# Down and output projections of a float32r macaron block: high and low weights side by side, one 512-column product for the high block

## The chip, the cores and the metric

One NeuronCore of a Trainium2 chip runs the whole kernel in one launch. The metric is device time in microseconds (us), the median of repeated executions. One further execution was recorded by the hardware profiler; its trace is what the rows below come from.

Engines are named as the profile names them: PE is TensorE's matmul side and PEld its weight loads, DVE is VectorE, ACT is ScalarE, POOL is GpSimd, SP is SyncE (here it only issues DMAs). A matmul takes a stationary block (the "weights" of PEld, up to 128x128) and streams a moving block of up to 512 columns past it.

## The reference

The input x is 4096 tokens of 256 channels. The block is `x + 0.5*FFN(LN(x))`, then `x + Attention(LN(x))`, then `x + 0.5*FFN(LN(x))` again. FFN is a mixture of 8 experts with top-2 routing and a capacity of 1228 rows per expert:

```python
h = einp2 @ w_c_fc + b_c_fc            # (1228 x 256) @ (256 x 1024), per expert
g = einp2 @ w_gate + b_gate
o = silu(h * g) @ w_c_proj + b_c_proj  # (1228 x 1024) @ (1024 x 256): the down projection
```

Attention is a gated linear recurrence over 16 heads of 64 channels, `S = a*S + k v^T`, `o = q S`, whose output is multiplied by `W_o` (1024 x 256): the output projection. All is float32.

## The kernel before

**Split precision.** Each float32 operand of a large product is split into a high part, rounded to the float32r type by an ACT copy, and a low part, the remainder, made by a DVE subtraction. A product of two such operands is three matmuls into the same PSUM bank: high x high, high x low, low x high. The helper `passes` (line 298) lists them in that order.

**Stages.** Round r=0: `route` (normalise, logits, top-2, scatter of rows into `expert_in` in HBM), then a loop over eight experts; then `attention`; then round r=1 with `route` and eight experts again; then `combine_last`, in which POOL gathers expert rows and DVE adds them into x, and SP stores x.

**One expert.** Its 1228 rows are three groups of 512, 512 and 204 rows. The second group is computed 384 or 512 wide (`wide1`), the third only if it holds rows (`last_group`); both are read at run time from `long`. `up` (line 552) makes 8 units per group, 12 matmuls each, into banks 0 to 3; ACT and DVE turn them into `s_hi` and `s_lo`. `down` (line 571) makes tiles of 128 rows: tile t has 4+4+2 = 10 numbers per expert (the last has 76 rows), and for each of the HJ=8 blocks j of the hidden axis it issues three matmuls with 256 columns each, 24 matmuls per tile, into columns 0 to 255 of bank 4 + t%2. The stationary block is the 128x128 block of `s_hi` or `s_lo`, the moving one 256 columns of `pr_hi` or `pr_lo`. The order on PE is `up` 0, `up` 1, `down` 0 (tiles 0 to 3), `up` 2 if it exists, `down` 1 tiles 0 and 1 (t = 4, 5), `turn` of the next expert's first rows (line 539), t = 6, then t = 7 only if `wide1`, then t = 8, 9 only if `last_group`, then the next expert's `up` 0.

**The bank's way back.** When a tile is done PE raises `y_done`; DVE's `y_out` (line 1205) adds bank and bias into `y_sb` (one addition, line 1212) and raises `y_copied`. PE needs that before it writes tile t+2 into the same bank (line 582); SP needs it to store the tile (line 357), and behind stores 0 to 3 SP issues the next expert's row loads (line 383). DVE's stream is in order. Behind tile 6 stand two `split_fc` subtractions (line 1165) and the two subtractions of `turned` (line 1177), and these raise `xt_split`, for which the next expert's first matmul waits (line 556); `y_out(7)` to `y_out(9)` come after them.

**Attention.** A loop over eight supertiles of 4 tiles of 128 tokens. At the end of each, `out_projection` (line 721) makes 4 tiles of 24 matmuls with 256 columns (8 head pairs g, three passes) into banks 3 and 4, and DVE's `add_output` (line 1374) adds each bank into x with one addition and raises `wo_added`. Then PE goes on with `values` of the next supertile (48 matmuls with 512 columns) and waits for the last `wo_added` behind them (line 763).

The weights sit in `halves`, a buffer of 32768 float32r per partition: `pr_hi` at 8192 and `pr_lo` at 10240; `wo` at 16384 and 18432.

Of the kernel before, what the change touches and what calls it, by code (L numbers as in the profile page):

```python
# [20 lines left out]
ALU = mybir.AluOpType  # L21
# [8 lines left out]
P = 128  # L30
T = 4096
C = 256
# [65 lines left out]
def macaron(nc, x_in, w_q, w_k, w_v, w_gate, b_gate, w_o, router_w, router_b,  # L98
            w_fc, b_fc, w_g, b_g, w_proj, b_proj, out):
    with ExitStack() as ctx:  # L100
# [39 lines left out]
        def part(t, at, *dims):  # L140
            n = 1
            for d in dims:
                n *= d
            v = t[:, at:at + n]
            names = "abc"[:len(dims)]
            if len(dims) == 1:
                return v
            return v.rearrange(f"p ({' '.join(names)}) -> p {' '.join(names)}",
                               **{names[i]: dims[i] for i in range(1, len(dims))})
# [13 lines left out]
        fc_hi, fc_lo, gw_hi, gw_lo = (part(halves, 2048 * i, KC, HID) for i in range(4))  # L163
        pr_hi, pr_lo = (part(halves, 2048 * i, HJ, C) for i in (4, 5))
        s_hi = [part(halves, 12288 + 8192 * i, HJ, 512) for i in range(2)]
# [40 lines left out]
                          for i in range(4))  # L206
        wo = [part(halves, 16384, NPAIR, C), part(halves, 18432, NPAIR, C)]
        xa = [part(halves, 20480, KC, SW), part(halves, 21504, KC, SW)]
# [44 lines left out]
        y_done = sem("y_done")  # L253
        y_copied = sem("y_copied")
        y_stored = [sem("y_stored0"), sem("y_stored1")]
# [18 lines left out]
        o_done, ot_hi_made, ot_split = sem("o_done"), sem("ot_hi_made"), sem("ot_split")  # L274
        wo_done, wo_added = sem("wo_done"), sem("wo_added")
        stored = sem("stored")
# [219 lines left out]
        def _(pe):  # L496
# [74 lines left out]
            def down(r, e, n, tiles=range(SUPER)):  # L571
                u = r * E + e
                buf = n % 2
                pe.wait_ge(s_split, u * UNITS + (n + 1) * HJ)
                if n == 0:
                    pe.wait_ge(proj_split, u * 4 + 4)
                for i, (o, m) in enumerate(GROUP_TILES[n]):
                    if i not in tiles:
                        continue
                    t = 4 * n + i  # L580
                    if t >= 2:
                        pe.wait_ge(y_copied, u * Y_TILES + t - 1)
                    ps = [(j, a, v) for j in range(HJ)
                          for a, v in passes((s_hi[buf], s_lo[buf]), (pr_hi, pr_lo))]
                    for k, (j, a, v) in enumerate(ps):
                        mm = pe.matmul(bank[4 + t % 2][0:m, 0:C], a[:, j, o:o + m], v[:, j, :],  # L586
                                       start=(k == 0), stop=(k == len(ps) - 1))
                    mm.then_inc(y_done, 1)
# [37 lines left out]
            def attention():  # L626
# [94 lines left out]
                def out_projection(s):  # L721
                    pe.wait_ge(ot_split, s * NPAIR + NPAIR)
                    for b in range(SUPER):
                        if b >= 2:
                            pe.wait_ge(wo_added, s * SUPER + b - 1)
                        ps = [(g, a, v) for g in range(NPAIR) for a, v in passes(ot, wo)]
                        for i, (g, a, v) in enumerate(ps):
                            m = pe.matmul(bank[3 + b % 2][:, 0:C], a[:, g, b * P:(b + 1) * P], v[:, g, :],  # L728
                                          start=(i == 0), stop=(i == len(ps) - 1))
                        m.then_inc(wo_done, 1)  # L730
# [57 lines left out]
        def _(act):  # L788
# [27 lines left out]
            def split_attention(n):  # L816
                w = (wq, wk, wz, wv, wo)[n]
                act.wait_ge(aw_staged[n], 16)
                copy(w[0].rearrange("p a n -> p (a n)"), raw_w[n]).then_inc(aw_hi_made, 1)

# [184 lines left out]
        def _(dve):  # L1005
# [161 lines left out]
            def split_attention(n):  # L1167
                w = (wq, wk, wz, wv, wo)[n]
                dve.wait_ge(aw_hi_made, n + 1)
                v.tensor_tensor(w[1].rearrange("p a n -> p (a n)"), raw_w[n],  # L1170
                                as_f32(w[0].rearrange("p a n -> p (a n)")), ALU.subtract).then_inc(aw_split, 1)

# [8 lines left out]
            def expert(r, e, last):  # L1181
# [23 lines left out]
                def y_out(t):  # L1205

                    n = t // 4 if t < 8 else 2
                    m = GROUP_TILES[n][t - 4 * n][1]
                    dve.wait_ge(y_done, u * Y_TILES + t + 1)

                    dve.wait_ge(y_stored[t % 2], (u * (Y_TILES // 2) + t // 2 + 1) * 16)
                    v.tensor_tensor(y_sb[0:m, t % 2, :], bank[4 + t % 2][0:m, 0:C], y_bias[0:m, :],  # L1212
                                    ALU.add).then_inc(y_copied, 1)

# [55 lines left out]
            def attention():  # L1270
# [103 lines left out]
                def add_output(s, b):  # L1374
                    i = s * SUPER + b
                    dve.wait_ge(wo_done, i + 1)
                    v.tensor_tensor(tile_of(x, i), bank[3 + b % 2][:, 0:C], tile_of(x, i),
                                    ALU.add).then_inc(wo_added, 1)

# [85 lines left out]
```

## Time and profile before

| what | value |
|---|---|
| median of 3 runs | 2385.33 us (2384.83 to 2389.75) |
| the profiled execution's own time | 2385.95 us |
| its span, first to last instruction | 2384.2 us |
| PE busy / PEld busy | 2025.1 us (85%) / 1799.6 us (75%) |
| DVE / ACT / POOL busy | 1263.0 us (53%) / 1130.6 us (47%) / 298.3 us (13%) |
| mean granted TensorE clock | 0.944 of full speed |
| matmuls, in all / of line 586 (down) / of line 728 (output projection) | 13967 / 3288 / 768 |

A row of a timeline gives the start, the duration, the engine, the line and operation, what it writes and reads, how many instructions were merged into the row, and in brackets how long the engine had been idle before and what released it. Merged instructions overlap: an instruction's duration includes its latency, so the distance between starts is what an engine pays for one. A matmul's "busy" time in a table by lines is the time its kind occupied the engine, while the mean of one is its latency.

### The profile page before, as it was taken

What the parts mean: (1) busy time and instruction counts of PE and PEld (TensorE: products, weight loads), DVE (VectorE), ACT (ScalarE), POOL (GpSimd) and SP (SyncE); (2) the same over time, 40 slices, a digit from 0 to 9 for tenths busy, and PEclk for the clock granted to TensorE, in tenths of its full rate; (3) what the DMA queues carried; (4) which work ended last, traced back from release to release, by engine and by line L of the source; (5) the groups of instructions that cost most, each with busy time, mean ns of one, the idle gap of its engine ahead of it and who ended that gap; (6) DMA issues with size and microseconds to landing.
All of it is one profiled execution on the core that took longest, in us unless ns stands there. A gap on an engine that the chain in (4) does not pass through costs nothing.

```text
span 2384.2 us, 38690 instructions
## 1 busy us (share of the span) xinstructions
PE 2025.1 (85%) x13967; PEld 1799.6 (75%) x13968; DVE 1263.0 (53%) x3160; ACT 1130.6 (47%) x2054; POOL 298.3 (13%) x332
## 2 busy tenths in 40 slices
PE   5169999999995989898988999983399999999990
PEld 5158889898985777787877788873398899988890
DVE  6345555555455647474564756545254545564544
ACT  1055566655453535354453644520366556665540
POOL 1720000000002101110010110006300000000226
PEclk9999999999997999999999999975699999999995
DMA  6242221222121000000000000002411221222224
GB/s 259 103 144 81 97 86 55 71 97 97 37 87 53 15 11 11 14 12 13 10 10 10 14 13 0 1 1 91 158 52 69 93 80 48 73 91 97 76 60 142
DMA packets 95402, 150.90 MB, mean 63 GB/s; under 512 B 9583, under 2 KB 76678, under 8 KB 94068
## 3 DMA queue, kind: packets, MB, share of 16 engines
q1 hardware_dynamic: 83008, 116.46, 14.3%
q0 software_dynamic: 12288, 32.91, 4.4%
q8 instruction: 81, 1.33, 0.2%
q14 instruction: 25, 0.20, 0.0%
HBM read 98.84 MB, written 51.15 MB: 63 GB/s over the span
## 4 chain that ended last, share of the span: by engine, by line
PE 66%; DVE 11%; PEld 7%; issue 6%; POOL 6%; ACT 2%; DMA 1%; PEldq 1%; DVEq 0%; POOLq 0%; SPq 0%; ACTq 0%
PE bank L567 27%; PE bank L586 12%; PE bank L638 5%; PE bank L728 4%; PEld bank L586 4%; POOL expert_in L436 4%; PE bank L662 4%; PEld bank L567 3%; PE bank L682 2%; DVE wide L1343 2%; PE bank L716 2%; POOL halves L443 2%; PE bank L531 2%; PE bank L708 2%; DVE wide L1366 1%
## 5 line engine op out<-in xcount | busy, mean ns | idle before, releaser
L567 PE MATMUL bank<-halves 128*128 128x512 f32 (+2 forms) x3744 | 770.4, 366 | 22.3 <-DVE halves L1177 22.3
L567 PEld LDWEIGHTS bank<-halves 128*128 128x128 f32 x3744 | 648.9, 191 | 128.0 <-issue 24.6
L586 PE MATMUL bank<-halves 128*128 128x256 f32 (+1 forms) x3288 | 403.2, 283 | 3.0 <-issue 3.0
L586 PEld LDWEIGHTS bank<-halves 128*128 128x128 f32 (+1 forms) x3288 | 397.3, 189 | 5.7 <-issue 4.8
L834 ACT ACTIVATE temp<-bank,bias_now 128x512 f32<-128x512 f32 (+1 forms) x312 | 200.3, 642 | 367.6 <-PE bank L567 367.3
L1190 DVE SCALAR_TENSOR_TENSOR temp<-bank,bias_fc,temp 128x512 f32<-128x512 f32 (+1 forms) x312 | 216.3, 693 | 225.9 <-ACT temp L834 222.4
L638 PE MATMUL bank<-halves 128*128 128x512 f32 x1152 | 290.4, 404 | 2.0 <-DVE halves L1317 2.0
L1197 DVE TENSOR_TENSOR halves<-temp,halves 128x512 fp32r<-128x512 f32 (+1 forms) x312 | 198.1, 635 | 126.6 <-ACT halves L790 123.5
L638 PEld LDWEIGHTS bank<-halves 128*128 128x128 f32 x1152 | 215.6, 192 | 51.1 <-DVE halves L1317 2.4
L790 ACT ACTIVATE halves<-temp 128x512 fp32r<-128x512 f32 (+1 forms) x313 | 184.9, 591 | 10.0
L443 POOL DMA_INDIRECT halves<-expert_out,read_slot x96 | 104.2, 1085 | 672.7 <-DMA expert_out<-rows 648.0
L1325 DVE TENSOR_TENSOR_SCAN wide<-wide,limit 128x64 f32<-128x64 f32 x512 | 100.6, 270 | 154.1 <-ACT wide L909 154.1
L1212 DVE TENSOR_TENSOR rows<-bank,rows 128x256 f32<-128x256 f32 (+1 forms) x160 | 66.9, 423 | 217.7 <-PE bank L586 191.6
L841 ACT ACTIVATE temp<-temp 128x512 f32<-128x512 f32 (+1 forms) x312 | 179.9, 577 | 0.2
L790 ACT ACTIVATE halves<-wide 128x512 fp32r<-128x512 f32 (+1 forms) x196 | 115.5, 644 | 116.7 <-DMA wide<-in_L_ffn_w_gate 99.0
L790 ACT ACTIVATE temp<-wide 64x256 f32<-64x256 f32 (+1 forms) x192 | 105.9, 551 | 130.7 <-DVE wide L1366 128.4
L790 ACT ACTIVATE halves<-bank 128x512 fp32r<-128x512 f32 (+1 forms) x176 | 89.4, 541 | 162.7 <-PE bank L548 127.6
L548 PE MATMUL bank<-ident,wide 128*128 128x128 f32 x320 | 43.3, 276 | 125.0 <-DMA wide<-expert_in 125.0
L436 POOL DMA_INDIRECT expert_in<-wide,temp x128 | 127.7, 998 | 145.0 <-issue 82.3
L548 PEld LDWEIGHTS bank<-ident,wide 128*128 128x128 f32 x320 | 38.0, 144 | 129.7 <-DMA wide<-expert_in 126.0
L1165 DVE TENSOR_TENSOR halves<-wide,halves 128x512 fp32r<-128x512 f32 x128 | 81.8, 685 | 86.2 <-ACT halves L790 78.1
L465 POOL COPY temp<-carry 128x384 f32<-128x384 f32 x64 | 32.3, 505 | 704.0 <-DVE wide L1343 704.0
(155 smaller groups left out, 2124.2 us busy)
## 6 DMA issues: line engine op xcount, KB each, us to landing
expert_out<-rows SPq DMA_DIRECT2D x144, 128.0 KB, 1.7
wide<-in_L_ffn_w_c_fc SPq DMA_DIRECT2D x16, 1024.0 KB, 5.4
wide<-in_L_ffn_w_gate SPq DMA_DIRECT2D x16, 1024.0 KB, 7.6
wide<-in_L_ffn_w_c_proj SPq DMA_DIRECT2D x16, 1024.0 KB, 5.4
wide<-expert_in SPq DMA_DIRECT2D x32, 512.0 KB, 4.9
expert_in<-halves SPq DMA_DIRECT2D x9, 1024.0 KB
x<-in_L_attn_x SPq DMA_DIRECT2D x4, 1024.0 KB, 9.3
out_x<-x SPq DMA_DIRECT2D x32, 128.0 KB, 2.5
```

The lines of the kernel that those rows point to most:

```text
L436: pool.indirect_dma_start(expert_in, bass.IndirectOffsetOnAxis(ap=write_slot[:, j:j + 1], axis=0), xn[:, i, :], None, bounds_check=ROWS - ...
L443: pool.indirect_dma_start(into, None, expert_out, bass.IndirectOffsetOnAxis(ap=read_slot[:, j:j + 1], axis=0)).then_inc(landed, 16)
L567: m = pe.matmul(bank[at + b][:, 0:w], a[:, kc, j * P:(j + 1) * P], v[:, kc, 0:w], start=(i == 0), stop=(i == len(ps) - 1))
L586: mm = pe.matmul(bank[4 + t % 2][0:m, 0:C], a[:, j, o:o + m], v[:, j, :], start=(k == 0), stop=(k == len(ps) - 1))
L638: m = pe.matmul(bank[at][:], a[:, kc, g * P:(g + 1) * P], v[:, kc, :], start=(i == 0), stop=(i == len(ps) - 1))
L662: m = pe.matmul(bank[5 + n % 2][:], a[:, kc, b * P:(b + 1) * P], v[:, kc, half * 512:(half + 1) * 512], start=(i == 0), stop=(i == len(ps) ...
L790: return nc.scalar.activation(o, i, ACT.Copy)
L834: nc.scalar.activation(g_sb[b][:, 0:w], bank[2 + b][:, 0:w], ACT.Identity, bias=bias_now[:, j:j + 1]).then_inc(g_copied, 1)
L841: nc.scalar.activation(hg[b][:, 0:w], hg[b][:, 0:w], ACT.Silu).then_inc(silu_made, 1)
L1190: v.scalar_tensor_tensor(hg[b][:, 0:w], bank[b][:, 0:w], bias_fc[:, bass.ds(col, 1)], g_sb[b][:, 0:w], ALU.add, ALU.mult).then_inc(hg_made, 1)
L1197: v.tensor_tensor(s_lo[buf][:, j, 0:w], hg[b][:, 0:w], as_f32(s_hi[buf][:, j, 0:w]), ALU.subtract).then_inc(s_split, 1)
L1325: ins = v.tensor_tensor_scan(gates, gates, limit[:], 0.0, ALU.add, ALU.min)
```

## The change

The high and low weights of the down projection are stored next to each other for each hidden block j (256 high columns, then 256 low), and so are those of the output projection for each head pair g. The high stationary block meets both in one matmul with 512 columns, which fills the whole bank: columns 0 to 255 collect high x high, columns 256 to 511 collect high x low. The low stationary block still meets the high weights with 256 columns, into columns 0 to 255. So a block j or g has two matmuls in place of three, with the same 768 columns in all. DVE reads both halves of the bank: it adds the first half to the bias (or to x), waits for that on a semaphore of its own, and adds the second half. `y_copied` and `wo_added` are raised by the second addition. The subtractions and copies that make the weights' parts keep their sizes; they write rows of 256 with a stride of 512.

```diff
-        pr_hi, pr_lo = (part(halves, 2048 * i, HJ, C) for i in (4, 5))
+        pr = part(halves, 8192, HJ, 2, C)
+        pr_hi, pr_lo = pr[:, :, 0, :], pr[:, :, 1, :]
...
-        wo = [part(halves, 16384, NPAIR, C), part(halves, 18432, NPAIR, C)]
+        wo_both = part(halves, 16384, NPAIR, 2, C)
+        wo = [wo_both[:, :, 0, :], wo_both[:, :, 1, :]]
...
-                    ps = [(j, a, v) for j in range(HJ)
-                          for a, v in passes((s_hi[buf], s_lo[buf]), (pr_hi, pr_lo))]
-                    for k, (j, a, v) in enumerate(ps):
-                        mm = pe.matmul(bank[4 + t % 2][0:m, 0:C], a[:, j, o:o + m], v[:, j, :],
-                                       start=(k == 0), stop=(k == len(ps) - 1))
+                    y_bank = bank[4 + t % 2]
+                    for j in range(HJ):
+                        pe.matmul(y_bank[0:m, :], s_hi[buf][:, j, o:o + m], pr[:, j, :, :].rearrange("p a n -> p (a n)"),
+                                  start=(j == 0), stop=False, skip_group_check=True)
+                        mm = pe.matmul(y_bank[0:m, 0:C], s_lo[buf][:, j, o:o + m], pr_hi[:, j, :],
+                                       start=False, stop=(j == HJ - 1), skip_group_check=True)
...
-                        ps = [(g, a, v) for g in range(NPAIR) for a, v in passes(ot, wo)]
-                        for i, (g, a, v) in enumerate(ps):
-                            m = pe.matmul(bank[3 + b % 2][:, 0:C], a[:, g, b * P:(b + 1) * P], v[:, g, :],
-                                          start=(i == 0), stop=(i == len(ps) - 1))
+                        o_bank = bank[3 + b % 2]
+                        for g in range(NPAIR):
+                            pe.matmul(o_bank[:], ot[0][:, g, b * P:(b + 1) * P],
+                                      wo_both[:, g, :, :].rearrange("p a n -> p (a n)"),
+                                      start=(g == 0), stop=False, skip_group_check=True)
+                            m = pe.matmul(o_bank[:, 0:C], ot[1][:, g, b * P:(b + 1) * P], wo[0][:, g, :],
+                                          start=False, stop=(g == NPAIR - 1), skip_group_check=True)
...
-                    v.tensor_tensor(y_sb[0:m, t % 2, :], bank[4 + t % 2][0:m, 0:C], y_bias[0:m, :],
-                                    ALU.add).then_inc(y_copied, 1)
+                    y, y_bank = y_sb[0:m, t % 2, :], bank[4 + t % 2]
+                    v.tensor_tensor(y, y_bank[0:m, 0:C], y_bias[0:m, :], ALU.add).then_inc(y_halved, 1)
+                    dve.wait_ge(y_halved, u * Y_TILES + t + 1)
+                    v.tensor_tensor(y, y_bank[0:m, C:2 * C], y, ALU.add).then_inc(y_copied, 1)
...
                     v.tensor_tensor(tile_of(x, i), bank[3 + b % 2][:, 0:C], tile_of(x, i),
+                                    ALU.add).then_inc(wo_halved, 1)
+                    dve.wait_ge(wo_halved, i + 1)
+                    v.tensor_tensor(tile_of(x, i), bank[3 + b % 2][:, C:2 * C], tile_of(x, i),
                                     ALU.add).then_inc(wo_added, 1)
```

## Rows read from the trace of the kernel before

**Rows 1.** The page: span, and each engine's busy time, share and instructions.
```profile
span 2384.2 us, 38690 instructions
PE 2025.1 (85%) x13967; PEld 1799.6 (75%) x13968; DVE 1263.0 (53%) x3160; ACT 1130.6 (47%) x2054; POOL 298.3 (13%) x332
```
**Rows 2.** The page: chain of work that ended last, by engine and by line.
```profile
PE 66%; DVE 11%; PEld 7%; issue 6%; POOL 6%; ACT 2%; DMA 1%; PEldq 1%; DVEq 0%; POOLq 0%; SPq 0%; ACTq 0%
PE bank L567 27%; PE bank L586 12%; PE bank L638 5%; PE bank L728 4%; PEld bank L586 4%; POOL expert_in L436 4%; PE bank L662 4%; PEld bank L567 3%; PE bank L682 2%; DVE wide L1343 2%; PE bank L716 2%; POOL halves L443 2%; PE bank L531 2%; PE bank L708 2%; DVE wide L1366 1%
```
**Rows 3.** Groups by line, PE: shapes, count, busy us, mean ns, idle before.
```profile
L586 PE MATMUL bank<-halves 128*128 128x256 f32 x3120 | 383.6, 284 | 3.0 <-issue 3.0
L728 PE MATMUL bank<-halves 128*128 128x256 f32 x768 | 96.1, 287 | 11.4 <-DVE halves L1371 11.4
L586 PE MATMUL bank<-halves 128*76 128x256 f32 x168 | 20.7, 278 | 0.0
```
**Rows 4.** Timelines: what follows tiles of 256, 512, 384 and 204 columns.
```profile
2317.78 0.42 DVE L1212 TENSOR_TENSOR rows<-bank,rows 128x256 f32<-128x256 f32 x1 [2.46 <-PE bank L586]
2320.66 0.42 DVE L1212 TENSOR_TENSOR rows<-bank,rows 128x256 f32<-128x256 f32 x1 [2.45 <-PE bank L586]
...
873.77 0.60 ACT L790 ACTIVATE wide<-bank 128x512 f32<-128x512 f32 x1 [0.76 <-PE bank L662]
875.13 0.60 ACT L790 ACTIVATE wide<-bank 128x512 f32<-128x512 f32 x1 [0.76 <-PE bank L662]
...
2062.13 0.69 ACT L834 ACTIVATE temp<-bank,bias_now 128x512 f32<-128x512 f32 x1 [0.20 <-PE bank L567]
2064.21 0.69 ACT L834 ACTIVATE temp<-bank,bias_now 128x512 f32<-128x512 f32 x1 [0.20 <-PE bank L567]
...
717.62 0.43 ACT L834 ACTIVATE temp<-bank,bias_now 128x204 f32<-128x204 f32 x1 [0.24 <-PE bank L567]
718.96 0.43 ACT L834 ACTIVATE temp<-bank,bias_now 128x204 f32<-128x204 f32 x1 [0.24 <-PE bank L567]
```
**Rows 5.** Lines 1212 and 1250: durations min/median/max; a dependent pair of line 1250.
```profile
L1212 DVE TENSOR_TENSOR rows<-bank,rows x160: 414/424/425, 194.8 to 2323.5; 128x256 f32<-128x256 f32 x144, 76x256 f32<-76x256 f32 x16
L1250 DVE SCALAR_TENSOR_TENSOR x<-halves,weight,x x64: 457/483/489, 750.3 to 1431.9; 128x256 f32 x56, 128x256 f32<-128x256 f32 x8
750.32 1.01 DVE L1250 SCALAR_TENSOR_TENSOR x<-halves,weight,x 128x256 f32<-128x256 f32 x2
```
**Rows 6.** Timeline, 278 to 281 us: from tile 6 to the next expert.
```profile
278.06 0.42 DVE L1212 TENSOR_TENSOR rows<-bank,rows 128x256 f32<-128x256 f32 x1 [2.21 <-PEq L620]
278.40 1.28 DVE L1165 TENSOR_TENSOR halves<-wide,halves 128x512 fp32r<-128x512 f32 x2
279.60 1.28 DVE L1177 TENSOR_TENSOR halves<-bank,halves 128x512 fp32r<-128x512 f32 x2
281.02 2.50 PE L567 MATMUL bank<-halves 128*128 128x512 f32 x5 [3.09 <-DVE halves L1177]
```
**Rows 7.** Waits of PE: us in total, times, longest.
```profile
PE bank L567 <- DVE halves L1177: 22.3, 11, 3.1
```
**Rows 8.** Stretches: busy us per engine, then granted clock (third value from the end).
```profile
280.60:284.00 3.40, 2.98 (x7) 2.41 (x8) 1.37 (x4) 0.00 (x0) 0.00 (x0) 0.50 0.23 77
347.10:353.90 6.80, 6.80 (x30) 5.65 (x31) 1.90 (x5) 1.72 (x3) 0.00 (x0) 1.00 0.35 103
2164.80:2171.60 6.80, 5.62 (x13) 4.45 (x14) 2.13 (x5) 0.10 (x1) 0.00 (x0) 0.50 0.25 72
```
**Rows 9.** Timelines behind the last projection of each of the three stages.
```profile
742.42 1.52 POOL L443 DMA_INDIRECT halves<-expert_out,read_slot  x1 [607.20 <-DMA expert_out<-rows]
1589.28 3.03 PE L509 MATMUL bank<-ident,wide 128*128 128x128 f32 x13 [5.59 <-DVE wide L1122]
2323.80 12.74 DVE L1261 SCALAR_TENSOR_TENSOR x<-wide,weight,x 128x256 f32<-128x256 f32 x32
2326.97 10.40 POOL L443 DMA_INDIRECT halves<-expert_out,read_slot  x1 [40.84 <-DMA expert_out<-rows]
```
**Rows 10.** Row loads of the next expert (line 334) and the turn they feed.
```profile
203.83 1.00 SPq L334 DMA_DIRECT2D wide<-expert_in  x2
DMA to landing us min/median/max: 4.6/4.9/5.3
208.79 0.93 PE L548 MATMUL bank<-ident,wide 128*128 128x128 f32 x7
```

More of the change, by code:

```diff
@@ L144, in part @@
             v = t[:, at:at + n]
-            names = "abc"[:len(dims)]
+            names = "abcd"[:len(dims)]
             if len(dims) == 1:
@@ L253, in macaron @@
         y_done = sem("y_done")
-        y_copied = sem("y_copied")
+        y_halved, y_copied = sem("y_halved"), sem("y_copied")
         y_stored = [sem("y_stored0"), sem("y_stored1")]
@@ L274, in macaron @@
         o_done, ot_hi_made, ot_split = sem("o_done"), sem("ot_hi_made"), sem("ot_split")
-        wo_done, wo_added = sem("wo_done"), sem("wo_added")
+        wo_done, wo_halved, wo_added = sem("wo_done"), sem("wo_halved"), sem("wo_added")
         stored = sem("stored")
@@ L818, in split_attention @@
                 act.wait_ge(aw_staged[n], 16)
-                copy(w[0].rearrange("p a n -> p (a n)"), raw_w[n]).then_inc(aw_hi_made, 1)
+                copy(w[0], raw_w[n].rearrange("p (a n) -> p a n", a=w[0].shape[1])).then_inc(aw_hi_made, 1)
             def turned(r, e, n):
@@ L1169, in split_attention @@
                 dve.wait_ge(aw_hi_made, n + 1)
-                v.tensor_tensor(w[1].rearrange("p a n -> p (a n)"), raw_w[n],
-                                as_f32(w[0].rearrange("p a n -> p (a n)")), ALU.subtract).then_inc(aw_split, 1)
+                v.tensor_tensor(w[1], raw_w[n].rearrange("p (a n) -> p a n", a=w[0].shape[1]),
+                                as_f32(w[0]), ALU.subtract).then_inc(aw_split, 1)
             def turned(r, e, n):
```

## The prediction

> **What bounds the kernel now.** I read the shares first: PE is busy for 85% of the span, DVE for 53% [rows 1]. The chain that ended last runs through PE and PEld for 73% of the span, and the two changed lines hold 20% of it (586: 12% and 4%, 728: 4%) [rows 2]. So time saved on PE in these lines is mostly time saved, and the question is how much each instruction pays beside its columns. The groups by line give the amount of work: 3120 + 168 matmuls in line 586, 768 in line 728, nearly without idle time before them (3.0 and 11.4 us) [rows 3]. At 24 a tile that is 137 down tiles and 32 output tiles, 169 in all. The counts also tell the experts apart: 168/24 = 7 tiles have 76 rows, so 7 of the 16 experts have a third group; 137 - 16*7 - 2*7 = 11 have tile 7; 9 experts have no third group, 4 of them with tile 7 and 5 without.
>
> **What one matmul costs.** A matmul's mean latency (284 ns) says nothing of this; the distance between tiles does. Down tiles of 24 matmuls with 256 columns follow each other at 2320.66 - 2317.78 = 2.88 us, 120.0 ns each. The value products are 6 matmuls with 512 columns in 1.36 us, 226.7 ns each. The units 384 wide, 12 matmuls in 2.08 us, pay 173.3 ns; those 204 wide, 12 in 1.34 us, pay 111.7 ns [rows 4]. From 256 to 384 to 512 the price rises by 53.3 ns for 128 columns each time, 0.417 ns a column, so a matmul pays 13.3 ns besides its columns (120.0 - 256*0.417). At 204 columns the line would give 98 ns, and the row says 112: something else, the next weight load most likely, holds it there. At 256 columns, 8 ns above that floor, the columns still decide.
>
> **What the change removes.** Three matmuls at 120.0 become one at 226.7 and one at 120.0: 360.0 becomes 346.7, 13.3 ns less for each of 8 blocks, 0.107 us a tile. All 169 tiles: 18.0 us. The trace has no stretch in which the two widths alternate, so this is bounded from both sides. At most nothing but columns is paid: 768*0.417 = 320 ns, 40 ns a block, 54 us in all. At least nothing is gained (360), if the wide product pays as much as the two it stands for; a loss would need a price above 226.7 for a 512-column matmul that has a weight load behind it, and line 662 is nothing but such matmuls. I take 346.7, since both its terms are the neighbouring rows' own prices for exactly these shapes.
>
> The Trainium skill ("TensorE: Matmul & The Clock Gate", section "Back-to-back issue gap") gives an isolated matmul N/2.4 + 2.5 ns, 109 ns for 256 columns and 216 for 512; by that the third instruction is worth 2.5 ns, 3.4 us in all. The rows stand 11 ns above it at both widths, so here the measured 13.3 decides.
>
> **What it adds on DVE, where covered.** One more addition per tile. The second one depends on the first: in line 1250's dependent pairs, two additions of 483 ns take 1.01 us together, so the second starts about 0.04 us after the first has ended; an addition of line 1212 takes 0.424 us [rows 5]. The pair therefore ends 0.46 us later than the single one did. Inside a run of tiles this costs nothing: PE needs the bank only after a whole further tile (2.77 us), the pair is back in about 1.1 us, and DVE had been idle for 2.45 us before each addition [rows 4]. Behind the third group's units and in the supertiles it is also covered: line 1377's last addition has the 48 value products (11 us) before PE waits for it. The copies and subtractions of the weights keep their element counts: nothing.
>
> **Where it is not covered.** (1) The nine expert boundaries without a third group. Behind tile 6 stand, in DVE's order, y_out(6), two subtractions of line 1165 and two of line 1177, and PE's next expert waits for the last: 278.06 to 280.88 on DVE, and PE goes on at 281.02 after 3.09 us [rows 6]. Of the eleven such waits [rows 7] two are the first experts of the rounds, nine are these. The additional 0.46 us lies fully in this chain: 9*0.46 = 4.1 us. In four of them PE does tile 7 meanwhile, and that tile's 0.107 us is lost in the longer wait: 0.4 us. (2) The ends of three stages: the gathers after round 0 wait for the last stored tile, PE's first transposes of round 1 wait for DVE, and DVE's 32 additions of line 1261 and POOL's gathers follow the very last tile [rows 9]. Each shifts by 0.46: 1.4 us. (3) SP issues the next expert's row loads behind store 3. Relative to the start of the four tiles, `y_copied` comes 0.46 later and tile 3 ends 0.43 earlier, so the loads are issued 0.03 later, while PE arrives at the turn six tiles, 0.64 us, earlier. The two loads were issued together at 203.83, a landing takes 4.6 to 5.3 us from issue, and PE turned the first at 208.79 without waiting [rows 10]. That is between no room at all and, since the first of the two should land well before the second, about 1 us. I cost it at nothing; without that room it is 9*0.67 = 6.0 us.
>
> **The sum.** 18.0 - 4.1 - 0.4 - 1.4 = 12.1 us less. The profiled execution's own 2385.95 becomes 2373.9. Its time is 0.6 us above the median shown, so the median 2385.33 becomes 2373.2.
>
> **The rivals.**
> *Slower, by the clock.* The nine boundary waits grow by 0.4 us, and some of them already cost more than their length: at 280.6 us, just behind a 3.1 us wait, the granted clock is 0.50 for 3.4 us, at 2164.8 for 6.8 us, while behind the same wait before 347.1 it stays at 1.00 [rows 8], and so it does behind the four waits of about 1 us. Now such stretches follow 4 of the 9 waits (three of 3.4 us, one of 6.8). A stretch at 1.2 GHz in place of 2.4 costs half its length, 8.5 us now. If the longer waits brought one of 6.8 us behind each of the nine, that would be 30.6 us: 22.1 more than now, 2395.3 us. The change turns slower once the added stretches sum to more than 24 us. For it: 4 of 5 long waits already have one. Against it: five of the nine are nearly all paid already, and the short four would still be under 1.5 us long.
> *Nothing saved per product.* If the wide product costs 240 between narrow ones, the 18.0 us vanish and the uncovered 5.5 us remain (no tile-7 loss): 2390.8. Against it are the rows of both widths; for it only that the mixed order is not in the trace. By the Trainium skill's formula named above, the saving would be 3.4 us and the time 2387.4, a little slower as well.
> *More saved.* If the 13.3 ns is only paid where a weight load is hardly covered, a load behind 512 columns could be free of it: 13 ns more a block, another 18 us, 2355. Against it: line 662 has only such loads and pays 13.3 all the same.
> *The gain is eaten at the boundaries.* If the row loads land as late as the bound in (3), the time is 2379.2; with one more stretch of half clock, 2380.9, within 0.2% of before.
> *The change doesn't do what it says,* for instance the count of line 586 does not fall by a third: then no term holds. I see nothing for it; the two halves of a pair of weights are adjacent, so one moving block of 512 columns is what line 662 already streams.
>
> **How the numbers follow.** Forecast (2373.2, within 5 us): 0.66. More saved (2355, or part of it, under 2368): 0.11. Eaten at the boundaries (2379 to 2381): 0.10. Nothing saved per product (2387 to 2391): 0.07. Slower by the clock: 0.06. What a measurement of this kernel can tell from no change is 0.2%, 4.8 us, so faster means under 2380.6. The forecast, more saved, and half of the eaten case are that: 0.82. The other half of that case, and parts of the two slower ones near their break-even points, give 0.08 for the same. Slower by over 0.2% (above 2390.1) or near it keeps 0.10. The range leaves out the two slower cases and most of the larger saving: 2366 to 2382.
>
> **What would show it.** Line 586 with 2192 matmuls and line 728 with 512. Down tiles at 2.77 us in place of 2.88: if 2.88 remains, nothing is saved per product; if 2.66 or less, more is. Lines 1212 and 1377 twice as many additions, the pair 0.88 us long. In the nine boundaries the chain from y_out(6) to the next expert's first matmul 0.46 us longer, and no new idle time before line 548; a DMA named there means point (3) was wrong. Stretches at half clock no more than about 5.1 us longer in sum behind those boundaries. The prediction falls if the tiles come at 2.77 and the time still does not: then a wait took the gain.

## The result and the profile after

The changed kernel takes 2345.63 us (median of 4 runs, 2343.08 to 2348.09); before, beside it, 2385.65 us. The ratio is 0.983 with a 95% interval of 0.9816 to 0.9843: 40 us less, where 12 were forecast, and outside the forecast range of 2366 to 2382.

The page of the changed kernel: its span, busy times, the queue that fetches instructions, and the costliest groups of the changed lines. Columns as in [rows 1] and [rows 3].

```profile
span 2341.3 us, 36178 instructions
PE 1999.5 (85%) x12615; PEld 1711.1 (73%) x12616; DVE 1343.4 (57%) x3352; ACT 1130.7 (48%) x2054; POOL 299.3 (13%) x332
...
q8 instruction: 33, 0.54, 0.1%
...
L589 PE MATMUL bank<-halves 128*128 128x512 f32 x1040 | 368.2, 398 | 3.1 <-issue 3.1
L591 PE MATMUL bank<-halves 128*128 128x256 f32 x1040 | 290.9, 280 | 0.0
```

The products are as announced: a wide and a narrow one where there were three, 1352 matmuls fewer against [rows 1]. PE's busy time fell by 26 us, though, and the span by 43. So much of the gain is time in which PE did nothing before, and by the stages it lies where few products changed. From the attention's first transpose to its last product it took 763.1 to 1583.4 us before, and takes 761.7 to 1542.6 now: 39 us less, with 32 of the 169 tiles. The sixteen experts together are 6 us shorter.

In the attention, one place differs. These are PE's rows of the kernel before around the end of a pass of the supertile loop, from the last value product to the next pass's first transpose; below them the loop's branch in PE's queue (durations min/median/max in ns), what the instruction queue brought in the whole run (packets, MB, share), and two windows (PE's busy time first, the granted clock third from the end).

```profile
881.73 1.54 PE L662 MATMUL bank<-halves 128*128 128x512 f32 x6
888.65 1.12 PE L671 MATMUL bank<-ident,wide 128*128 128x128 f32 x4 [5.38 <-issue]
...
L772 PEldq COMPARE_BRANCH  x7: 83/3397/3859, 881.8 to 1498.1; - x7
...
q8 instruction: 81, 1.33, 0.2%
...
883.00:888.60 5.60, 0.28 (x2) 0.00 (x0) 0.52 (x2) 0.60 (x1) 0.00 (x0) 0.96 0.02 6
990.60:997.40 6.80, 4.33 (x23) 3.58 (x24) 1.15 (x3) 1.89 (x4) 0.00 (x0) 0.50 0.01 2
```

The same views of the changed kernel:

```profile
878.78 1.77 PE L667 MATMUL bank<-halves 128*128 128x512 f32 x7
881.32 0.65 PE L676 MATMUL bank<-ident,wide 128*128 128x128 f32 x4 [0.77 <-ACT wide L798]
...
L780 PEldq COMPARE_BRANCH  x7: 76/208/226, 879.1 to 1460.9; - x7
```

Before, the branch back took 3.3 to 3.9 us, PE stood still for 4.9 to 5.6 us with "issue" as the reason, which means that the profile shows nothing it waited for, and the clock was then granted at 0.50 for 3.4 or 6.8 us. From the start of the last value product to the start of the next pass's first transpose, five of the passes had a gap of 5.77, 5.51, 5.40, 5.30 and 5.94 us; each is 1.15 us now. That is 22.1 us. A half-clock stretch begins in each of the five gaps, 30.6 us long in all, and costs more. How much more shows beside run e5 below, which has the same products and does not stall: there the loop's first six passes, from the first pass's first transpose to the seventh's, take 583.0 us (787.07 to 1370.02); here they take 616.1 (786.84 to 1402.97). That is 33.2 us, 11 of them for the clock, and the forecast had no term for any of it. In one pass, from 880 to 984 us, q8 brought 9 packets of 16384 bytes before; in the changed kernel's loop it brings none.

### The profile page after: what moved, and what is told of

Read it like the earlier page. It is cut to its first block, busy times and chain, and to the rows that moved or that the text cites. A ratio compares the mean times of both kernels' runs of the same rounds, so it can differ in the third digit from the quotient of the medians.

```text
span 2341.3 us, 36178 instructions
## 1 busy us (share of the span) xinstructions
PE 1999.5 (85%) x12615; PEld 1711.1 (73%) x12616; DVE 1343.4 (57%) x3352; ACT 1130.7 (48%) x2054; POOL 299.3 (13%) x332
## 4 chain that ended last, share of the span: by engine, by line
PE 69%; DVE 11%; POOL 6%; issue 5%; PEld 4%; ACT 2%; DMA 2%; PEldq 1%; SPq 0%; DVEq 0%; POOLq 0%; ACTq 0%
PE bank L569 30%; PE bank L589 8%; PE bank L643 5%; PE bank L591 4%; POOL expert_in L438 4%; PE bank L667 4%; PE bank L733 3%; DVE wide L1353 2%; PE bank L687 2%; PE bank L721 2%; POOL halves L445 2%; PEld bank L569 2%; PE bank L533 2%; PE bank L713 2%; DVE wide L1376 1%
## 5 line engine op out<-in xcount | busy, mean ns | idle before, releaser
L569 PE MATMUL bank<-halves 128*128 128x512 f32 (+2 forms) x3744 | 771.9, 366 | 24.9 <-DVE halves L1185 24.9
L589 PE MATMUL bank<-halves 128*128 128x512 f32 (+1 forms) x1096 | 387.7, 397 | 3.1 <-issue 3.1
L591 PE MATMUL bank<-halves 128*128 128x256 f32 (+1 forms) x1096 | 306.5, 280 | 0.0
L643 PE MATMUL bank<-halves 128*128 128x512 f32 x1152 | 285.3, 399 | 2.0 <-DVE halves L1327 2.0
L589 PEld LDWEIGHTS bank<-halves 128*128 128x128 f32 (+1 forms) x1096 | 203.2, 185 | 55.2 <-issue 5.9
L591 PEld LDWEIGHTS bank<-halves 128*128 128x128 f32 (+1 forms) x1096 | 204.3, 186 | 0.4
```

Of the source, the lines that this page charges most:

```text
L569: m = pe.matmul(bank[at + b][:, 0:w], a[:, kc, j * P:(j + 1) * P], v[:, kc, 0:w], start=(i == 0), stop=(i == len(ps) - 1))
L589: pe.matmul(y_bank[0:m, :], s_hi[buf][:, j, o:o + m], pr[:, j, :, :].rearrange("p a n -> p (a n)"), start=(j == 0), stop=False, skip_group ...
L591: mm = pe.matmul(y_bank[0:m, 0:C], s_lo[buf][:, j, o:o + m], pr_hi[:, j, :], start=False, stop=(j == HJ - 1), skip_group_check=True)
L643: m = pe.matmul(bank[at][:], a[:, kc, g * P:(g + 1) * P], v[:, kc, :], start=(i == 0), stop=(i == len(ps) - 1))
```

## The experiments

Times are medians. e1 to e4 ran on one chip, and so did e5 to e8, e9 to e12 and e13 to e15, each beside the kernel before. "Ahead" and "in the loop" count PE instructions.

| run | median us | ratio to before, 95% | q8 packets | gaps at the loop's end, us |
|---|---|---|---|---|
| e1 output projection alone | 2348.49 | 0.9824 to 0.9860 | 36 | 1.15 to 1.33 |
| e2 down projection alone | 2347.58 | 0.9811 to 0.9844 | 34 | 1.15 |
| e3 change, 32 instructions more in the loop | 2350.25 | 0.9823 to 0.9856 | 34 | 1.15 |
| e4 change, wide products first | 2342.72 | 0.9796 to 0.9829 | 33 | 1.15 |
| e5 before, 64 instructions more ahead | 2350.64 | 0.9827 to 0.9867 | 37 | 1.15 |
| e6 e2, 64 instructions more ahead | 2384.83 | 0.9977 to 1.0002 | 88 | 5.31 to 5.92 |
| e7 change, 128 ahead, 64 in the loop | 2348.42 | 0.9815 to 0.9852 | 34 | 1.15 |
| e8 e4, other order on DVE | 2323.77 | 0.9715 to 0.9750 | 33 | 1.15 |
| e9 change, 64 ahead, 64 in the loop | 2388.51 | 0.9989 to 1.0040 | 88 | 5.45 to 5.87 |
| e10 change, one addition (high x low left out of the result) | 2342.22 | 0.9787 to 0.9865 | 33 | 1.15 |
| e11 e5 again | 2350.61 | 0.9816 to 0.9896 | 37 | 1.15 |
| e12 the change again | 2346.68 | 0.9800 to 0.9878 | 33 | 1.15 |
| e13 e5, other order on DVE | 2334.63 | 0.9750 to 0.9808 | 37 | 1.15 |
| e14 change, other order on DVE | 2323.73 | 0.9708 to 0.9766 | 33 | 1.15 |
| e15 e8 again | 2323.48 | 0.9698 to 0.9757 | 33 | 1.15 |

### One half of the change at a time: e1 and e2

e1 keeps the three narrow products in `down` and the one addition in `y_out`; e2 does the same for `out_projection` and `add_output`.

> Only the output projection is changed (wide products, second addition of line 1377's kind); the down projection stays with three products of 256 columns and one addition. Theory 'code': what saved most of the time is that the supertile loop on PE became 64 instructions shorter (1588 to 1524), so that its code need not be fetched again in each pass. Then the five gaps of 5.3 to 5.9 us between values and turn_keys shrink to 1.15 us, the packets of the instruction queue q8 fall from 81 to about 33, the half-clock stretches behind those gaps are gone, and the time is about 35 to 39 us below before: 2347 to 2351 us. Rival 'products': the saving is spread over all 169 tiles, so 32 of 169 tiles carry a fifth of it, 8 us: 2378 us.

> Only the down projection is changed; the output projection stays as before, and with it the length of the supertile loop (1588 instructions). Theory 'code': the five long gaps stay, q8 stays near 81 packets, and only the down tiles' gain less the boundary cost is left: 4 to 8 us less, 2378 to 2382 us. Rival 'products': four fifths of the saving, about 32 us less: 2353 us.

Measured: 2348.49 and 2347.58 us. Each half alone brings nearly the whole gain, and the two do not add up. e1 met the expectation of "code", e2 refuted it in the form it had: its supertile loop is the old one, instruction for instruction, and still does not stall. "Products" fell with both.

### Filling up the loop: e3

```diff
+                            for _ in range(8):
+                                pe.wait_ge(consts_made, CONSTS)
                             ps = [(kc, a, v) for kc in range(KC) for a, v in passes(xa, wv)]
```

> The changed kernel with 64 further waits on PE in each pass of the supertile loop, eight ahead of each value product, on a semaphore that has long reached its value: the loop is 1588 instructions again, all products as changed. Theory 'code': the gaps of 5 us come back, q8 goes back to about 80 packets, time 2345.6 + 30 to 37 = 2376 to 2383 us. Rival 'products': the waits are dispatched while PE still has products queued; at about 0.05 us each they are 3.2 us per pass of dispatch, hidden behind 11 us of value products, so the time stays at 2346 us, 2372 at the most if nothing hid them (8 * 3.2), with gaps of 1.15 us between values and turn_keys all the same.

Measured: 2350.25 us, no stall. The fillers were half of what was meant: two waits go into one instruction (EVENT_SEMAPHORE 47 a pass in place of 15), so the loop was 1556 instructions long, not 1588, and 32 more stood ahead of it, in the copy of `values` that is made once before the loop. Inconclusive on the length, and it stays as a weaker piece of evidence.

### Moving the loop: e5 and e6

What e1, e2 and the change share is fewer instructions in PE's program, in the loop or ahead of it. The next pair changes only where the loop begins.

```diff
+                for _ in range(128):
+                    pe.wait_ge(consts_made, CONSTS)
                 pe.wait_ge(aw_split, 5)
                 pe.wait_ge(att_cleared, ATT_CLEARS)
                 turn_x(0)
```

> The kernel before, not one product or addition changed, with 64 more PE instructions (128 waits on a semaphore long reached, two to an instruction) once, ahead of the attention, where PE idles for 24 us anyway. Undoing either half of the change alone kept nearly the whole gain (e1, e2), though e2 leaves the attention's program as it was before; so theory 'length of the loop' has fallen, and what e1, e2 and the change share is that PE's program is shorter ahead of or in the supertile loop. Theory 'place': code comes in pieces of 16384 bytes, and the loop of the kernel before straddles one more piece than PE can keep because of where it begins; moving it by 64 instructions is enough. Then the branch of the supertile loop takes 0.2 us in place of 3.4, the five gaps fall to 1.15 us, q8 falls to about 35 packets, and the time falls by 30 to 37 us: 2351 to 2358 us. Rival 'products': nothing of the products changes, so 2386 to 2388 us.

> Run e2 with the same 64 PE instructions ahead of the attention. The down change took 320 PE instructions out ahead of the loop; 64 put back makes that 256, one piece of 16384 bytes if an instruction has 64 bytes, so the loop has its old length and its old place within a piece. Theory 'place': the gaps of 5 us, the 3.4 us branches and 80 packets of q8 come back: 2347.6 + 30 to 37 = 2378 to 2385 us. Rivals ('products', or 'shorter program' in general: PE's program is still 256 instructions shorter than before): no change, 2348 us.

Measured: 2350.64 and 2384.83 us. The kernel before, with all its products and 64 idle instructions more, is 36.4 us faster than itself. e2, with the same 64, loses 37.3 us again (e2 ran on another chip; the kernel before took 2388.08 us there and 2387.02 here). Both rivals predicted no change and are refuted. The rows of e5 and then of e6, the end of a pass and the branch:

```profile
880.78 2.68 PE L662 MATMUL bank<-halves 128*128 128x512 f32 x11
884.23 0.65 PE L671 MATMUL bank<-ident,wide 128*128 128x128 f32 x4 [0.77 <-ACT wide L792]
...
L774 PEldq COMPARE_BRANCH  x7: 76/208/226, 882.0 to 1464.9; - x7
...
q8 instruction: 37, 0.61, 0.1%
```

```profile
879.62 1.99 PE L667 MATMUL bank<-halves 128*128 128x512 f32 x8
886.90 1.12 PE L676 MATMUL bank<-ident,wide 128*128 128x128 f32 x4 [5.29 <-issue]
...
L779 PEldq COMPARE_BRANCH  x7: 83/3487/3759, 880.1 to 1501.7; - x7
...
q8 instruction: 88, 1.44, 0.2%
```

In e6 all six branches back stall (gaps of 5.67, 5.71, 5.48, 5.66, 5.92 and 5.31 us).

The arithmetic behind the two expectations: ahead of the attention PE's program holds the expert twice (the loop's copy and the last expert's). The down change takes 8 matmuls and 8 weight loads out of each of 10 tiles, 160 instructions a copy, 320 in all.
The Trainium skill ("Runtime: NRT & Kernel Launch", section "Instruction fetch mechanics") says that PE holds 128 KiB of instructions, 2048 of them, refilled in blocks of 16 KiB. The packets and the 256 instructions of e6 agree with the block; a loop of 8 blocks and the next one fetched ahead would be one too many, which fits the 9 packets a pass; this is an inference, no run varies the number of blocks by itself. The same section says that a taken branch whose target is outside the current window of two pages forces a fetch. Here the traces disagree: in e5 the branch goes back over 1588 instructions in 0.2 us and nothing is fetched.

### The stall put back into the changed kernel: e7 and e9

> The changed kernel, all products as changed, with 64 PE instructions ahead of the attention and 64 in the loop (e3's 64 waits were only 32 instructions, as two go into one). The loop is as long as before, 1588 instructions, and begins where e6's does within a piece. Theory 'place': the gaps come back: 2350 + 30 to 37 = 2380 to 2387 us. Rival 'products': 2350 to 2353 us, as in e3.

Measured: 2348.42 us, no stall, as the rival said. The kernel was not what its expectation described: the fillers ahead of the value products also stand in the copy of `values` that is made once ahead of the loop, so the loop began 64 instructions too late. e9 has those 64 alone ahead (`range(16)` in e3's edit, without e5's).

> Run e7 without the 64 instructions ahead. e7 was built wrongly for its purpose: its fillers also stand in the value products that are made once ahead of the loop, so the loop began another 64 instructions later than e6's. Here these are the only ones ahead: 320 out and 64 in, as in e6, the loop 1588 instructions long, all products as changed. Theory 'place': the 3.4 us branches, gaps above 5 us and some 80 packets of q8 come back, 2346 + 35 = 2381 us. Rival (the wide products are what spares the loop its stall): 2348 us as in e7.

Measured: 2388.51 us, with all products of the change. The branch and the gap of e9:

```profile
L782 PEldq COMPARE_BRANCH  x7: 83/3408/3793, 882.8 to 1503.6; - x7
...
879.70 4.49 PE L669 MATMUL bank<-halves 128*128 128x512 f32 x19
889.42 1.11 PE L678 MATMUL bank<-ident,wide 128*128 128x128 f32 x4 [5.24 <-issue]
```

e7 has 64 idle instructions more than e9 and is 40 us faster (they ran on two chips; the kernel before took 2387.02 and 2387.22 us beside them). Within a piece e9's loop begins where that of the kernel before does, and e7's where e5's does. This settles it: neither the wide products nor the program's total length decides, but where the loop begins and ends. Once it does not stall, the rest of the change is small.

### The change's own worth: e11 and e12, e10

> Run e5's kernel again, beside the changed kernel on the same chip: the comparison of the change with what it should have been compared with, a kernel before whose loop does not stall. Theory: the change's own worth is the products' gain less the boundaries' cost, 3 to 8 us, so this one is 3 to 8 us slower than the changed kernel. Rival: the stretches of half clock decide, and the two are equal within 2 us.

> The changed kernel itself, as the partner of e9 to e11 on their chip: 2343 to 2349 us.

> The changed kernel without DVE's second addition in both projections (the high x low part in the bank's second half is left out of the result). Theory: it costs 0.46 us where PE waits for DVE, that is at the five boundaries without tile 7 and at the ends of three stages, 3.7 us, perhaps with a half-clock stretch or two: 2 to 6 us faster than the changed kernel run beside it. Rival (the addition delays every tile's bank): 169 * 0.46, tens of microseconds faster.

Measured on one chip: 2350.61 us for the kernel before without the stall, 2346.68 for the change, 2342.22 for the change with one addition. The change itself is worth 3.9 us, just clear of the spread (2346.6 to 2355.2 against 2344.0 to 2347.8 us; the means differ by 4.4, with a 95% interval of 3.9 either way). The second addition costs 4.5 (3.5 either way), within what was expected, and does not delay the banks.

### The order of the products: e4

```diff
                         pe.matmul(y_bank[0:m, :], s_hi[buf][:, j, o:o + m], pr[:, j, :, :].rearrange("p a n -> p (a n)"),
                                   start=(j == 0), stop=False, skip_group_check=True)
+                    for j in range(HJ):
                         mm = pe.matmul(y_bank[0:m, 0:C], s_lo[buf][:, j, o:o + m], pr_hi[:, j, :],
```

> The changed kernel with the products of a tile in another order: the eight wide ones first, then the eight narrow ones, in the down and in the output projection. In the changed kernel the alternating pairs take 347 ns in some runs of tiles and 353 in others (wide 231 to 241, narrow 112 to 120), so four tiles take 11.29 us where 11.08 was forecast. Theory 'alternation': a load behind a wide product and one behind a narrow product do not come at an even pace, and this costs up to 7 ns a pair; grouped, a wide product costs 226.7 and a narrow one 120, a tile 2.774 us always, and about 169 * 8 * 4 ns = 5 us are saved: 2341 us. Rival: the 6 ns belong to the wide product into a bank that is being added up; then four tiles stay at 11.29 us and the time at 2345.6.

Output tiles of one supertile as DVE's additions follow them, in the changed kernel and then in e4:

```profile
859.95 0.42 DVE L1387 TENSOR_TENSOR x<-bank,x 128x256 f32 x1 [1.20 <-PE bank L736]
862.78 0.42 DVE L1387 TENSOR_TENSOR x<-bank,x 128x256 f32 x1 [1.95 <-PE bank L736]
865.58 0.42 DVE L1387 TENSOR_TENSOR x<-bank,x 128x256 f32 x1 [1.92 <-PE bank L736]
868.41 0.42 DVE L1387 TENSOR_TENSOR x<-bank,x 128x256 f32 x1 [1.95 <-PE bank L736]
```

```profile
860.95 0.42 DVE L1389 TENSOR_TENSOR x<-bank,x 128x256 f32 x1 [1.19 <-PE bank L738]
863.74 0.42 DVE L1389 TENSOR_TENSOR x<-bank,x 128x256 f32 x1 [1.91 <-PE bank L738]
866.52 0.42 DVE L1389 TENSOR_TENSOR x<-bank,x 128x256 f32 x1 [1.90 <-PE bank L738]
```

Alternating, a tile takes (868.41 - 859.95)/3 = 2.82 us, grouped (866.52 - 860.95)/2 = 2.79; the sum had 2.77 against 2.88. In the experts with a third group there are twelve runs of four down tiles that `up` follows (tiles 0 to 3, or 6 to 9): from first product to that `up` they take 11.51 us before, 11.30 in the mean after (11.19 to 11.34) and 11.19 grouped (11.14 to 11.26).

The changed kernel has a second pace, though, and it is the forecast one. These are the first products of tiles 0 and 3, in an expert with two groups and then in one with three:

```profile
257.52 0.39 PE L589 MATMUL bank<-halves 128*128 128x512 f32 x1
265.85 0.39 PE L589 MATMUL bank<-halves 128*128 128x512 f32 x1
...
395.01 0.39 PE L589 MATMUL bank<-halves 128*128 128x512 f32 x1
403.48 0.40 PE L589 MATMUL bank<-halves 128*128 128x512 f32 x1
```

Three tiles take 8.33 us there, 2.77 each, and 8.47 here, 2.82 each. So alternating by itself costs nothing: grouping saves 0.04 us on a tile of the slow pace and loses 0.02 on one of the quick pace. "Alternation" holds for the slow runs alone. In time e4 was 3 us faster than the change had been, but e15 against e14, on one chip, shows 0.2 us, where 2 to 4 were expected. Grouping is not shown to be worth anything that a run can tell.

### The order on DVE at the expert boundary: e8, e13 to e15

```diff
                 for t in range(4, Y_TILES):
-                    if not last and t < 8:
+                    if not last and t < 7:
                         split_fc(u * 8 + 8, 2 * (t - 4))
                         split_fc(u * 8 + 8, 2 * (t - 4) + 1)
-                    if not last and t == 7:
+                    if not last and t == 6:
+                        split_fc(u * 8 + 8, 6)
+                        split_fc(u * 8 + 8, 7)
                         turned(r, e + 1, 0)
```

> Run e4 with DVE's order at the expert boundary changed: the last two subtractions of the next expert's weights (line 1165's kind) and those of its turned rows (line 1177's) come before y_out(6) in place of after it. Theory: the nine waits of 1.0 and 3.8 us between down and the next up are y_out(6) and what stands behind it on DVE, not anything PE waits for by itself. Then they fall to under 0.5 us: 5 * 3.5 + 4 * 0.8 = 21 us, and the half-clock stretches behind them go too, 5 to 8 us: 2342.7 - 26 = 2317 us. Rival: the turned rows come late by themselves (ACT's copies behind the turn), and the waits shrink only by the 0.9 us of y_out(6): 2342.7 - 8 = 2335 us.

> Run e5's kernel (three narrow products, one addition, loop moved so that it does not stall) with DVE's order at the expert boundary as in e8. Theory: the change's own gain is 9 us of products, of which the boundaries without tile 7 and the ends take 3.7 us and stretches of half clock some more. With the boundaries reordered, e8's gain there (five waits 2.5 us shorter, and no half clock behind them) is had here too: 2350.6 - 19 = 2332 us. Rival (the reordering only repairs what the second addition costs): 2350.6 - 5 = 2346 us.

> The changed kernel with DVE's boundary order as in e8, products alternating as in the change. Theory: 6 to 8 us faster than e13 (the 9 us of products less the ends of three stages), and 2 to 4 us slower than e15 (the alternation): 2326 us. Rival: equal to e13 within 2 us, then what looked like the products' gain was something else.

> Run e8's kernel again as the partner of e13 and e14 on their chip: 2320 to 2326 us.

Measured: e8 2323.77 us, e13 2334.63, e14 2323.73, e15 2323.48. e8 is between its two expectations: the five boundaries without tile 7 fell from 3.83 to 1.36 or 1.42 us from start to start, but the four with tile 7 stayed at 1.0 or below, so there DVE had not been what PE waited for; e14's trace puts these four waits (2.7 us) down to "issue", with a 0.2 us branch of PE in them. The boundary in the changed kernel and in e14; there the subtractions of line 1185 end at 278.00, with y_out(6) behind them:

```profile
278.94 0.42 DVE L1221 TENSOR_TENSOR rows<-bank,rows 128x256 f32<-128x256 f32 x1 [1.88 <-PEq L625]
279.40 0.42 DVE L1223 TENSOR_TENSOR rows<-bank,rows 128x256 f32<-128x256 f32 x1
279.74 1.28 DVE L1173 TENSOR_TENSOR halves<-wide,halves 128x512 fp32r<-128x512 f32 x2
280.94 1.28 DVE L1185 TENSOR_TENSOR halves<-bank,halves 128x512 fp32r<-128x512 f32 x2
282.36 1.42 PE L569 MATMUL bank<-halves 128*128 128x512 f32 x5 [3.55 <-DVE halves L1185]
```

```profile
276.72 1.28 DVE L1185 TENSOR_TENSOR halves<-bank,halves 128x512 fp32r<-128x512 f32 x2
278.21 2.98 PE L569 MATMUL bank<-halves 128*128 128x512 f32 x12 [1.08 <-DVE halves L1185]
```

No stretch of half clock follows these boundaries in e8, e13, e14 or e15. e13 is 16 us under e11 (on another chip) and shows that the reordering is worth most of its gain in the old kernel too; in the changed one it is 23 (e12 to e14, on the same two chips). e14 against e13 is the change with that boundary cost gone: 10.9 us, where 6 to 8 were expected. e14 is as fast as e15 with the simpler order of products: 23 us under e12, 63 under the kernel before.

## Why the prediction was wrong

**The chain.** That PE bounds the kernel was right, and so was that time saved there in these lines is saved. The step that failed is the sum, 18.0 - 4.1 - 0.4 - 1.4: it counts a removed instruction only by its price in the stream of products. It looked at the changed lines alone and put at nothing, without a reason, what a shorter program does to PE's idle time "issue", 6% of the chain [rows 2]. The stall stood in the trace of before: five waits of 4.9 to 5.6 us at line 671 with no releaser, branches of 3.3 to 3.9 us, 81 packets on q8. A term for it, or a rival "PE's program gets shorter and the loop comes to lie otherwise", was missing altogether; that term is 36 to 37 us by the medians of e5 and e6, three times the forecast gain. In the profiled executions the passes lose 33.2 us with five stalls (before against e5) and 37.2 with six (e6 against e2, and e9 against e7). It has nothing to do with what the change is about, and 64 idle instructions buy it too.

**The products (18.0 us in the sum).** Mechanism right, size wrong. The prices at one width held: 2.88 us a tile before [rows 4], about 227 ns for 512 columns. A pair of the two widths took the forecast 346.7 ns in some runs of tiles (230 and 116 or 117) but 353 in others (233 to 241 and 113 to 120), where 346.7 was taken always. All stretches of `down` together, each up to PE's next work and the last of each round up to its last product, take 419.5 to 419.7 us in three profiles with three products a block (before, e5, e11) and 412.1 to 412.3 in two of the change (its own, e12). With the 2.6 us of longer waits below added back the products save 10.0 us; e13 against e14, where the waits are alike, gives 409.6 - 399.3 = 10.3. That is 0.07 us a tile, not 0.107. The output tiles of the first seven passes take 81.3 and 79.8 us, 0.054 a tile, 1.7 for all 32. So the term is some 11.9 us, between its two bounds (nothing, and 54 us). Why the pace has two values is open.

**The second addition.** The pair takes what was worked out: starts 0.46 us apart, 279.40 after 278.94. At the five boundaries without tile 7 PE's wait grew from 3.37 to 3.83 us, exactly 0.46. At the four with tile 7 it hardly grew (1.03, 0.99, 1.00, 0.75 became 1.06, 1.06, 1.00, 0.98), because most of that time was not DVE's, as e8 and e14 show. So the term of 4.1 + 0.4 us was 2.6, as PE's waits for line 1185 say, 24.9 us in place of 22.3 [rows 7]. The additions within runs of tiles were covered, as said. Of the ends of stages (1.4) the first costs nothing: PE's wait ahead of the attention is 24.3 us before and 24.2 after. The second is 0.60 (5.59 [rows 9] became 6.19), the third 0.47 by the start of POOL's gathers, 1.1 together. e10 gives 4.5 us for all uncovered places, the sum had 5.9.

**The row loads (3).** No new idle time ahead of the turn: costing it at nothing was right.

**The own gain together.** 11.9 - 2.6 - 1.1 = 8.2 us by the traces, where the sum said 12.1. e11 against e12 measured 3.9, and 8.2 is at the upper end of its interval (4.4 in the means, 3.9 either way). With the boundaries reordered the sum is 11.9 - 1.1 = 10.8; e13 against e14 measured 10.9 (10.6 in the means, 2.4 either way). What spreads the times is the half clock: two profiles of one and the same kernel, e5 and e11, have spans of 2345.4 and 2351.6 us, and e11's stands at half clock for 23.8 us behind the expert boundaries against e5's 6.8, and for 10.2 us more at 1535 us.

**The rivals.** "More saved" named the direction, for a reason that is refuted: no matmul went free of its 13 ns. "Slower by the clock" had the clock's place in mind at the expert boundaries; there the half-clock stretches sum to 13.6 and 20.4 us in two profiles of the changed kernel (its own, e12), against 17.0, 6.8 and 23.8 in three with the same boundaries as before (before, e5, e11). So the longer waits are not shown to bring more of them. The clock did matter in the loop, where it stood at half for 30.6 us and cost about 11. The range was missed because of the stall alone: the change's own gain, 3.9 to 8.2 us, would have given an estimated 2377 to 2381 us, inside it.

What stays open: in the kernel before one of six branches back did not stall, in e6 all six did; and two executions of the kernel before, 2364.05 and 2370.70 us beside e9 to e15, are far below its others without a trace to say why. How many pieces PE keeps is inferred: three builds stall, all at one place within a piece, and those of the same length that do not (e2, e5, e7) are at two others. The places between were not tried.

## What to carry to other kernels

Before costing a change to a long unrolled program, look for idle time that has no releaser, for long branches, and for packets on the instruction queue inside a loop: any edit that adds or removes instructions can switch such a stall on or off, and a few idle instructions ahead of the loop tell whether it does. Compare a change then with a kernel before that does not stall: here 40 us looked like the gain, and 4 to 11 were. On an in-order engine, put what another engine's next stage waits for ahead of the work that only frees a buffer.

## What the runs showed of the hardware

A PE loop of 1588 instructions ran without a fetch at three places in the program (e2, e5, e7; e5's and e7's are 256 instructions apart) and stalled at one place and 256 instructions away from it (before, e6, e9), with 9 fetches of 16384 bytes a pass. A stall costs 4.1 to 4.8 us at the branch, then 3.4 or 6.8 us stand at half clock, 6.2 to 6.6 us of time in all. Two waits on semaphores go into one PE instruction (e3: 64 waits, 32 instructions more). Matmuls of 512 and 256 columns in turn run at 347 ns a pair in some runs of tiles, the sum of what each width pays by itself (226.7 and 120.0), and at 353 in others.
